# First stage of a fused attention and expert kernel: the slots a body later, the choice ahead of the shared product, the scatter calls regrouped behind the last root

## The chip, the cores and the metric

The kernel runs on one core of one Trainium2 chip. The metric is the device time of one execution in microseconds; lower is better. The core has five engines with a queue of instructions each: TensorE (PE in the profile; its weight loads are PEld), VectorE (DVE), ScalarE (ACT), GpSimd (POOL) and SyncE (SP, which here only issues DMA transfers). An engine works through its queue in order. It meets the others only at semaphores.

## The reference, cut to what matters

```python
x = x + xattn0(layernorm(x), ctx)      # softmax(q ctx^T) ctx, q = x W^T + b
x = x + ffn0(layernorm(x))             # shared expert + routed top-1 of 8 experts
x = x + xattn1(layernorm(x), ctx, ctx) # softmax attention with projected k, v
x = x + ffn1(layernorm(x))             # 8 binary trees of depth 7: silu(logits) on the taken path

# ffn0, x of (8192, 128):
logits = x @ gate_w                    # (8192, 8)
top_id, score = argmax(logits), sigmoid(max(logits))
routed = swiglu(x * score; expert top_id)
out = swiglu(x; shared) + routed
```

There are 64 batches of 128 rows of 128 numbers, all in fp32; the context has 120 keys for each batch.

## The kernel before, in words

The batches are worked in 16 groups of 4. The first stage (`phase_a`) does the first attention, the shared expert, the router's logits, and the projections that the third step needs. It is a software pipeline of 19 bodies, f = 0 to 18. Body f works for four groups at once: it starts group f (statistics, keys), does the attention of group g = f - 1, the shared expert's first product for group l = f - 2, and its second product for m = f - 3. Every engine has its own `a_body`, and the order of the calls in it is the order in that engine's queue. Nothing is reordered by a scheduler. `PS` is the PSUM memory, in 8 banks of 512.

The routed expert is done in two halves of 8 groups (32 tiles of 128 rows) each. For a half, these steps follow each other:

- `choose_tops` and `choose_experts` on DVE turn the logits into a one-hot of the chosen expert (`top`, `lead`, `best`, `onehot`).
- `a_count` on PE multiplies it with a triangle and with ones: how many rows stand ahead of a row, and in each tile.
- `a_first_slots` on DVE finds where each expert's rows begin, `a_slots` turns that into `POS`, the place of every row in a list sorted by expert, and signals `placed`.
- `score` on ACT takes the sigmoid of `top` and signals `scored`. `scale(k)` multiplies the rows of group k by it: for group 0 on POOL, for 1 to 7 on ACT (`SCALED_IN` says in which body), for 8 to 15 on ACT in `scale_late`. SP's `load_rows` brings those rows from DRAM into four buffers (`xsa`, `xsb`), used again and again, and into four late ones.
- `scatter` on POOL writes one tile of 128 rows to its places in `x_sorted` with an indirect DMA. There are 32 such calls for the first half in bodies 12 to 17, between the other work of POOL, and 32 for the second half behind `placed` 2.

POOL also takes the reciprocal root of the variances (`rstd`, the rows `ve` and `rs`), twice for each group; DVE's `normalise` waits for it. In body 16 there is no group f, and the only root is that of group 15's second norm.

The second stage runs the sorted rows, 20 units of 4 tiles, through the experts. SP loads unit r with `r_load` into `xs_in`; units 0 and 1 are loaded once every scatter of the first half has landed (`all_scattered(sp, HG)`). In body 18 PE turns unit 0 (`r_turn(0, 0)`) behind the last group's shared product (`s_down`) and ahead of `a_count(1)`, so the second half's counts, slots and scatters stand behind it too. The third stage does the second attention and the trees, in a loop over the 16 groups.

The table `ROUTES` names the router's step of a body: tops in body 7, experts in body 8 (`choose0`), both for the next quarter in body 10 (`choose1`), counts in body 11 (`count`). `CALLS` holds the numbers of the scatter calls. The first half of a body's calls stands between its two roots, the other half behind the second root. A buffer of rows is loaded again only when its four scatters have landed, and SP waits for that in its queue.

## Time and profile before

| What | Value |
|---|---|
| three runs, median (lowest to highest) | 837.2 us (835.5 to 839.71) |
| profiled execution | 840.62 us |
| its span | 837.4 us, 3.2 us less |
| PE busy | 785.9 us, 94% of the span |
| DVE, ACT, POOL busy | 650.4, 558.8, 251.1 us |
| first stage ends, first sorted unit turned on PE | 219.95 us after the span's start |

The profile is one execution. The chain of waits follows the work that ended last back to the start. The timeline lists the instructions of an engine with start and duration, where instructions of one kind are merged (x4), and in brackets how long the engine was idle before, and what released it. "issue" is a release that the profile can't name.

### The profile page before, as it was taken

The page shows a single profiled execution, that of the slowest core. Times are in us where ns is not written, and L with a number is a line of the kernel's source. Part 1 is how long each engine was busy: PE and PEld are TensorE (multiplying, and loading weights), DVE is VectorE, ACT ScalarE, POOL GpSimd, SP SyncE. Part 2 cuts the span into 40 slices and gives each one's busy share as a digit, 9 for nine tenths or more (in the row PEclk, how much of TensorE's full clock was granted, in tenths as well). Part 3 has the DMA queues.
Part 4 walks back from the last instruction along what each step waited for, and adds up shares of the span by engine and source line. Part 5 has one row for each costly group of instructions (what it writes and reads, how often), then busy time and mean ns, then how long its engine had stood idle before and what let it go on. Part 6 is the DMA issues. An engine that isn't in the chain of part 4 may idle for free.

```text
span 837.4 us, 15003 instructions
## 1 busy us (share of the span) xinstructions
PE 785.9 (94%) x4424; PEld 635.5 (76%) x4464; DVE 650.4 (78%) x1730; ACT 558.8 (67%) x1007; POOL 251.1 (30%) x293
## 2 busy tenths in 40 slices
PE   5899997897878899999999999999999999999997
PEld 4788776776768899967777777777777777777775
DVE  5888889887824467778888888888888888888774
ACT  3577667685524434467777778678777777877765
POOL 2332322666265225112321331242133133211000
PEclk9999999999879899999999999999999999999999
DMA  6337784562523334100000000000000000000000
GB/s 170 87 112 197 200 238 135 165 176 72 161 85 105 92 110 115 51 25 11 26 27 0 25 25 0 25 25 19 6 25 25 0 25 25 16 11 13 13 1 25
DMA packets 91175, 55.79 MB, mean 67 GB/s; under 512 B 13439, under 2 KB 87799, under 8 KB 90999
## 3 DMA queue, kind: packets, MB, share of 16 engines
q1 hardware_dynamic: 75440, 41.29, 17.6%
q0 software_dynamic: 4096, 8.40, 3.5%
q10 hardware_dynamic: 11591, 5.50, 2.4%
q8 instruction: 25, 0.41, 0.2%
q14 instruction: 23, 0.19, 0.1%
HBM read 32.23 MB, written 22.94 MB: 66 GB/s over the span
## 4 chain that ended last, share of the span: by engine, by line
PE 76%; DVE 10%; ACT 7%; issue 4%; another core or an unknown queue 2%; DMA 0%; DVEq 0%; ACTq 0%; SPq 0%
PE PS L870 7%; PE PS L1124 7%; PE PS L855 7%; PE PS L1146 7%; PE PS L1148 7%; PE PS L1147 6%; PE PS L1126 6%; PE PS L1125 6%; PE PS L1068 4%; PE PS L1135 4%; PE PS L878 3%; PE PS L1133 2%; PE PS L1051 2%; PE PS L1036 2%; DVE xn L1205 2%
## 5 line engine op out<-in xcount | busy, mean ns | idle before, releaser
L812 ACT ACTIVATE sil<-PS,b_in_c 128x512 f32<-128x512 f32 x256 | 162.2, 685 | 92.2 <-PE PS L1133 60.7
L1591 DVE TENSOR_TENSOR sil_l<-sil,sil_h 128x512 fp32r<-128x512 f32 x256 | 164.8, 686 | 48.5 <-ACT sil_h L820 48.5
L542 POOL TENSOR_TENSOR ve<-mv,eps 128x4 f32<-128x4 f32 x64 | 19.7, 309 | 444.1 <-DVE mv L1199 442.6
L820 ACT ACTIVATE sil_h<-sil 128x512 fp32r<-128x512 f32 x224 | 128.9, 631 | 0.0
L1146 PE MATMUL PS<-sil_h,wout_l 128*128 128x512 f32 x256 | 118.8, 464 | 1.7 <-DVE sil_l L1591 1.6
L1124 PE MATMUL PS<-x4T_h,win_l 128*128 128x512 f32 x256 | 102.4, 400 | 0.9 <-ACT sil L812 0.4
L1148 PE MATMUL PS<-sil_h,wout_h 128*128 128x512 f32 x256 | 100.6, 393 | 0.0
L1147 PE MATMUL PS<-sil_l,wout_h 128*128 128x512 f32 x256 | 100.2, 391 | 0.0
L1126 PE MATMUL PS<-x4T_h,win_h 128*128 128x512 f32 x256 | 100.0, 391 | 0.0
L1125 PE MATMUL PS<-x4T_l,win_h 128*128 128x512 f32 x256 | 99.9, 390 | 0.0
L1575 DVE TENSOR_SCALAR dec<-PS,b_in_c 128x512 bf16<-128x512 f32 x128 | 95.4, 745 | 3.9 <-PE PS L1126 2.1
L870 PE MATMUL PS<-xsT,w_now 128*128 128x128 f32 x624 | 80.2, 282 | 3.4 <-issue 1.9
L604 POOL DMA_INDIRECT ys<-y_sorted,idx x64 | 72.0, 1125 | 27.8 <-issue 15.1
L870 PEld LDWEIGHTS PS<-xsT,w_now 128*128 128x128 f32 x624 | 76.0, 198 | 5.3 <-issue 4.7
L544 POOL TENSOR_TENSOR rs<-ve,neg_half 128x4 f32<-128x4 f32 x64 | 70.7, 1105 | 5.0
L769 ACT ACTIVATE sg<-PS 128x512 f32<-128x512 f32 (+1 forms) x40 | 23.4, 586 | 63.3 <-PE PS L870 45.6
L1194 DVE BATCH_NORM_STATS2 st<-X 128x6 f32<-128x128 f32 (+1 forms) x256 | 55.6, 280 | 9.5 <-DMA X<-in_x 4.5
L1265 DVE COPY w_now<-WGU 128x512 f32 x78 | 30.8, 436 | 41.0 <-PE PS L870 23.5
L1146 PEld LDWEIGHTS PS<-sil_h,wout_l 128*128 128x128 f32 x256 | 48.3, 189 | 18.7 <-DVE sil_l L1591 4.1
L1124 PEld LDWEIGHTS PS<-x4T_h,win_l 128*128 128x128 f32 x256 | 48.0, 188 | 16.5 <-issue 3.9
L1148 PEld LDWEIGHTS PS<-sil_h,wout_h 128*128 128x128 f32 x256 | 48.0, 188 | 11.2
L1126 PEld LDWEIGHTS PS<-x4T_h,win_h 128*128 128x128 f32 x256 | 48.0, 188 | 10.5
(174 smaller groups left out, 1575.1 us busy)
## 6 DMA issues: line engine op xcount, KB each, us to landing
x_sorted<-zeros SPq DMA_DIRECT2D x4, 1280.0 KB, 6.8
xs_in<-x_sorted SPq DMA_DIRECT2D x20, 256.0 KB
y_sorted<-yo ACTq DMA_DIRECT2D x18, 256.0 KB
X<-in_x SPq DMA_DIRECT2D x16, 256.0 KB
rows<-xn SPq DMA_DIRECT2D x16, 256.0 KB
out<-res SPq DMA_DIRECT2D x16, 256.0 KB
ctxT<-in_ctx_t SPq DMA_DIRECT2D x16, 240.0 KB
ctx_rows<-in_ctx_kv SPq DMA_DIRECT2D x16, 240.0 KB
```

The lines of the kernel that those rows point to most:

```text
L604: pool.indirect_dma_start(tile(ys[u], j), None, y_sorted[half], bass.IndirectOffsetOnAxis(ap=idx[:, u, j:j + 1], axis=0)).then_inc(y_in[u] ...
L812: act.activation(tile(sil[p % 2], c, W), bank(2 * (p % 2) + c), ACT.Silu, bias=b_in_c[:, 2 * p + c:2 * p + c + 1]).then_inc(t_silu, 1)
L820: act.activation(tile(sil_h[p % 2], c, W), tile(sil[p % 2], c, W), ACT.Copy).then_inc(t_hi, 1)
L870: i = pe.matmul(tile(bank(1 + 2 * v + t), n), tile(w_now[v], 2 * FC * t + n), tile(xsT[u], 2 * v + t), start=True, stop=True)
L1124: pe.matmul(dst, lo, x4T_h, start=True, stop=False, skip_group_check=True)
L1125: pe.matmul(dst, hi, x4T_l, start=False, stop=False, skip_group_check=True)
L1126: i = pe.matmul(dst, hi, x4T_h, start=False, stop=True, skip_group_check=True)
L1146: pe.matmul(bank(4), lo, act_h, start=(p == 0 and c == 0), stop=False)
L1147: pe.matmul(bank(4), hi, act_l, start=False, stop=False)
L1148: pe.matmul(bank(4), hi, act_h, start=False, stop=(p == TREES - 1 and c == 1)).then_inc(t_out, 1)
L1575: dve.tensor_scalar(dec[p % 2], bank(2 * (p % 2)), b_in_c[:, 2 * p:2 * p + 1], 0.0, ALU.add, ALU.is_gt).then_inc(t_dec, 1)
L1591: dve.tensor_tensor(tile(sil_l[p % 2], c, W), tile(sil[p % 2], c, W), tile(sil_h[p % 2], c, W).bitcast(F32), ALU.subtract).then_inc(t_lo, 1)
```

## The change

- `a_slots(0)` leaves the end of body 11 (route `count`) and stands in body 12 (new route `slots`), behind DVE's first `normalise` and ahead of the attended rows (`X<-PS,srec,X`).
- `score(0)` on ACT and the scaling of group 0 on POOL move from body 11 to body 12. `scale` on ACT waits for `scored` as well.
- In bodies 7, 8 and 10 DVE chooses ahead of the shared expert's product (`s_act<-s_act,PS`), not behind it; in body 10 the tops stand ahead of it and the experts behind.
- `CALLS` is now a table of three numbers for a body: the calls from the first to the second stand between the roots, those up to the third behind the second root. The calls of bodies 12 to 17 are 3, 6, 6, 6, 6, 5 (before 6, 6, 6, 6, 6, 2).
- In body 16 all six calls stand behind the root.
- POOL's wait for `zeroed` and `placed` stands behind the scaling of group 0. ACT scales group 2 in body 13 (before 12) and group 5 in body 15 (before 14).

```diff
-        ROUTES = {HG - 1: "choose0", HG: "choose0", HG + 2: "choose1", HG + 3: "count", NG + 1: "pack", NG + 2: "all"}
+        ROUTES = {HG - 1: "choose0", HG: "choose0", HG + 2: "choose1", HG + 3: "count", HG + 4: "slots",
+                  NG + 1: "pack", NG + 2: "all"}
-        CALLS = [0, 6, 12, 18, 24, 30, 32]
-        SCALED_IN = {HG + 4: (1, 2), HG + 5: (3,), HG + 6: (4, 5), HG + 7: (6,), HG + 8: (7,)}
+        CALLS = [(0, 0, 3), (3, 6, 9), (9, 12, 15), (15, 18, 21), (21, 21, 27), (27, 32, 32)]
+        SCALED_IN = {HG + 4: (1,), HG + 5: (2, 3), HG + 6: (4,), HG + 7: (5, 6), HG + 8: (7,)}
@@ POOL, a_body
-                if calls and calls[0] == 0:
-                    pool.wait_ge(zeroed, 16 * 4)
-                    pool.wait_ge(placed, 1)
-                half = (len(calls) + 1) // 2
-                for t in calls[:half]:
+                for t in range(calls[0], calls[1]):
                     scatter(t, 0, HG)
...
-                for t in calls[half:]:
-                    scatter(t, 0, HG)
-                if route == "count":
+                if route == "slots":
                     pool.wait_ge(scored, 1)
                     scale(0)
+                    pool.wait_ge(zeroed, 16 * 4)
+                    pool.wait_ge(placed, 1)
+                for t in range(calls[1], calls[2]):
+                    scatter(t, 0, HG)
@@ ACT, scale and a_body
+                act.wait_ge(scored, 1)
...
+                    if route == "slots":
                         score(0)
@@ DVE, a_body
+                if route == "slots":
+                    a_slots(0)
                 if g is not None:
                     dve.wait_ge(a_rec, g + 1)
...
+                if route == "choose0":
+                    choose_tops(0) if f == HG - 1 else choose_experts(0)
+                if route == "choose1":
+                    choose_tops(1)
                 if l is not None:
                     dve.wait_ge(s_sil, l + 1)
                     dve.tensor_tensor(s_act, s_act, PS[:, 6 * 512:8 * 512], ALU.mult).then_inc(s_act_d, 1)
-                if route == "choose0":
-                    choose_tops(0) if f == HG - 1 else choose_experts(0)
                 if route == "choose1":
-                    a_choose(1)
-                if route == "count":
-                    a_slots(0)
+                    choose_experts(1)
```

DVE's queue from the end of body 11 into body 12, before (`first_slot` ends `a_first_slots`; `slot` to `POS` is `a_slots`; `nmax` opens body 12; the last row is the attended rows):

```order
L1428 TENSOR_SCALAR first_slot<-first_slot 128x8 [waits route_step]
L1349 TENSOR_TENSOR s_act<-s_act,PS 128x1024 [waits s_sil,route_step]
L1435 TENSOR_TENSOR slot<-upto,first_slot 128x256
L1436 TENSOR_TENSOR lead<-ahead,slot 128x256 [waits route_step]
L1439 CAST POS<-posf 128x32 [waits route_step]
L1283 TENSOR_REDUCE nmax<-PS 128x4 [waits a_s_ps]
L1205 TENSOR_SCALAR xn_79<-X,mv,rs 128x128 [waits a_rs2,a_rows,a_x2T_ps]
L1205 TENSOR_SCALAR xn<-X,mv,rs 128x128 [waits a_rs1,a_xnT_ps]
L1330 SCALAR_TENSOR_TENSOR X<-PS,srec,X 128x128 [waits a_pv_ps,a_rec]
```

The same place in the changed kernel:

```order
L1431 TENSOR_SCALAR first_slot<-first_slot 128x8 [waits route_step]
L1356 TENSOR_TENSOR s_act<-s_act,PS 128x1024 [waits s_sil,route_step]
L1284 TENSOR_REDUCE nmax<-PS 128x4 [waits a_s_ps]
L1206 TENSOR_SCALAR xn_79<-X,mv,rs 128x128 [waits a_rs2,a_rows,a_x2T_ps]
L1206 TENSOR_SCALAR xn<-X,mv,rs 128x128 [waits a_rs1,a_xnT_ps]
L1438 TENSOR_TENSOR slot<-upto,first_slot 128x256
L1439 TENSOR_TENSOR lead<-ahead,slot 128x256 [waits route_step]
L1442 CAST POS<-posf 128x32 [waits route_step]
L1333 SCALAR_TENSOR_TENSOR X<-PS,srec,X 128x128 [waits a_pv_ps,a_rec]
```

The slots have moved from in front of `nmax` to a place behind the body's second `normalise`. The line numbers of the changed kernel are a few higher or lower.

POOL's queue from the second root of body 15 to the second half's first call, before (`xsa` and `xsb` are the row buffers; with their own numbers):

```order
L542 TENSOR_TENSOR ve<-mv,eps 128x4 [waits a_mv2]
L566 DMA x_sorted0<-xsa1_61,POS 5120x128 [waits k_act] x3
L566 DMA x_sorted0<-xsb0_68,POS 5120x128 [waits k_act] x3
L542 TENSOR_TENSOR ve<-mv,eps 128x4 [waits a_mv2]
L544 TENSOR_TENSOR rs<-ve,neg_half 128x4 [waits a_ve2]
L566 DMA x_sorted0<-xsb0_68,POS 5120x128 [waits k_act]
L566 DMA x_sorted0<-xsb1_69,POS 5120x128 [waits k_act] x4
L566 DMA x_sorted1<-xsa0_60,POS 5120x128 [waits placed,k_late]
```

The same place in the changed kernel:

```order
L543 TENSOR_TENSOR ve<-mv,eps 128x4 [waits a_mv2]
L567 DMA x_sorted0<-xsa0_60,POS 5120x128 [waits k_act] x2
L567 DMA x_sorted0<-xsa1_61,POS 5120x128 [waits k_act]
L543 TENSOR_TENSOR ve<-mv,eps 128x4 [waits a_mv2]
L545 TENSOR_TENSOR rs<-ve,neg_half 128x4 [waits a_ve2]
L567 DMA x_sorted0<-xsa1_61,POS 5120x128 [waits k_act] x3
L567 DMA x_sorted0<-xsb0_68,POS 5120x128 [waits k_act] x4
L567 DMA x_sorted0<-xsb1_69,POS 5120x128 [waits k_act] x4
L567 DMA x_sorted1<-xsa0_60,POS 5120x128 [waits placed,k_late]
```

The last root (the later row `ve<-mv,eps` with a_mv2) had 1 + 4 calls of the first half behind it, and three calls in front of it in its own body. Now it has 3 + 4 + 4 calls behind it and none in front in its body.

## Rows read from the trace of the kernel before

**Rows 1.** Page, chain that ended last: share of the span by engine
```profile
PE 76%; DVE 10%; ACT 7%; issue 4%; another core or an unknown queue 2%; DMA 0%; DVEq 0%; ACTq 0%; SPq 0%
```

**Rows 2.** Timeline, DVE, bodies 8, 11, 12: start, duration (us), line, operation, [idle before]
```profile
91.72 1.22 DVE L1349 TENSOR_TENSOR s_act<-s_act,PS 128x1024 f32<-128x1024 f32 x1 [0.94 <-ACT s_act L730]
...
93.93 0.66 DVE L1283 TENSOR_REDUCE nmax<-PS 128x4 f32<-128x480 f32 x1
...
141.74 0.17 DVE L1427 TENSOR_TENSOR first_slot<-tile_end,tiles_f 128x8 f32<-128x8 f32 x1
141.94 1.07 DVE L1428 TENSOR_SCALAR first_slot<-first_slot 128x8 f32<-128x8 f32 x1
...
144.18 0.42 DVE L1435 TENSOR_TENSOR slot<-upto,first_slot 128x256 f32<-128x256 f32 x1
...
146.28 0.65 DVE L1283 TENSOR_REDUCE nmax<-PS 128x4 f32<-128x480 f32 x1
...
149.76 0.69 DVE L1278 TENSOR_TENSOR X<-X,PS 128x512 f32<-128x512 f32 x1 [0.50 <-PE PS L878]
...
154.44 1.13 DVE L1330 SCALAR_TENSOR_TENSOR X<-PS,srec,X 128x128 f32<-128x128 f32 x4 [1.46 <-PE PS L977]
```

**Rows 3.** The same, PE, at the start of bodies 8, 9, 12
```profile
95.67 0.66 PE L855 MATMUL PS<-WA,xn 128*128 128x128 f32 x4 [0.87 <-DVE xn L1205]
...
107.77 0.66 PE L855 MATMUL PS<-WA,xn 128*128 128x128 f32 x4 [0.56 <-DVE xn L1205]
...
143.98 1.04 PE L916 MATMUL PS<-ctxT,W0C 128*128 128x480 f32 x2 [1.80 <-ACT KT L679]
...
148.01 0.66 PE L855 MATMUL PS<-WA,xn 128*128 128x128 f32 x4 [2.10 <-DVE xn L1205]
```

**Rows 4.** The same, ACT: body 11, body 14, routed stage
```profile
138.45 1.28 ACT L653 ACT_TABLE_LOAD   x1
...
139.88 0.58 ACT L723 ACTIVATE xnT<-PS 128x512 f32<-128x512 f32 x1
...
176.38 1.28 ACT L659 ACTIVATE xsa<-xsa,SCORE 128x128 f32<-128x128 f32 x4 [0.46 <-DMA xsa<-rows]
...
241.01 0.60 ACT L769 ACTIVATE sg<-PS 128x512 f32<-128x512 f32 x1 [6.58 <-remote]
...
272.59 0.60 ACT L769 ACTIVATE sg<-PS 128x512 f32<-128x512 f32 x1 [7.18 <-remote]
```

**Rows 5.** The same, POOL: score scaling, last root, scatter calls
```profile
141.94 1.04 POOL L551 TENSOR_TENSOR xsa<-xsa,SCORE 128x512 f32<-128x512 f32 x1
...
205.93 0.20 POOL L542 TENSOR_TENSOR ve<-mv,eps 128x4 f32<-128x4 f32 x1 [4.18 <-DVE mv L1199]
...
207.45 1.03 POOL L566 DMA_INDIRECT x_sorted<-xsb,POS  x1 [0.20 <-issue]
...
212.58 0.96 POOL L566 DMA_INDIRECT x_sorted<-xsb,POS  x1 [0.30 <-issue]
```

**Rows 6.** The same, SP's queue: a row load, first sorted loads
```profile
173.19 0.45 SPq L466 DMA_DIRECT2D xsa<-rows  x1
...
214.99 0.91 SPq L501 DMA_DIRECT2D xs_in<-x_sorted  x2
```

**Rows 7.** Tile late_rows, loads issued behind these: time to landing
```profile
DMA to landing us min/median/max: 5.3/5.5/5.8
```

**Rows 8.** Timeline, PE, end of first stage, start of the second
```profile
216.91 3.25 PE L878 MATMUL PS<-SD,s_act 128*128 128x128 f32 x16 [2.06 <-DVE s_act L1349]
219.95 1.06 PE L855 MATMUL PS<-WA,xs_in 128*128 128x128 f32 x4
...
221.75 2.02 PE L870 MATMUL PS<-xsT,w_now 128*128 128x128 f32 x16
...
246.98 3.75 PE L870 MATMUL PS<-xsT,w_now 128*128 128x128 f32 x16 [1.14 <-DVE ract L1514]
```

**Rows 9.** Windows: length, busy PE, PEld, DVE, ACT, POOL, granted clock, DMA share, GB/s
```profile
216.00:226.00 10.00, 8.94 (x59) 8.17 (x59) 7.76 (x23) 6.48 (x14) 0.00 (x0) 0.83 0.91 249
```

More of the change, by code:

```diff
@@ L359, in phase_a @@
                 body(stage(f), stage(f - 1), stage(f - 2), stage(f - 3), f % 2,
-                     range(CALLS[k], CALLS[k + 1]) if 0 <= k < len(CALLS) - 1 else (), ROUTES.get(f),
+                     CALLS[k] if 0 <= k < len(CALLS) else (0, 0, 0), ROUTES.get(f),
                      SCALED_IN.get(f, ()))
@@ L567, in scatter, with a_body @@
                                         tile(rows_of(k), t % G), None).then_inc(scattered[v], 16)
-            def a_body(f, g, l, m, u, calls=(), route=None, rows=()):
+            def a_body(f, g, l, m, u, calls=(0, 0, 0), route=None, rows=()):
                 if f is not None:
                     rstd(0, f, a_mv1, a_ve1, a_rs1)
-                if calls and calls[0] == 0:
-                    pool.wait_ge(zeroed, 16 * 4)
-                    pool.wait_ge(placed, 1)
-                half = (len(calls) + 1) // 2
-                for t in calls[:half]:
+                for t in range(calls[0], calls[1]):
                     scatter(t, 0, HG)
@@ L687, in take_gates, with a_body @@
                 act.activation(LGT[at:at + 32, :], bank(2, W, 32), ACT.Copy).then_inc(a_gT, 1)
-            def a_body(f, g, l, m, u, calls=(), route=None, rows=()):
+            def a_body(f, g, l, m, u, calls=(0, 0, 0), route=None, rows=()):
                 if m is not None and route != "all":
@@ L916, in project_keys, with a_body @@
                 pe.matmul(bank(0, KW), W0C[:, :], ctxT[u], start=True, stop=True).then_inc(a_k0_ps, 1)
-            def a_body(f, g, l, m, u, calls=(), route=None, rows=()):
+            def a_body(f, g, l, m, u, calls=(0, 0, 0), route=None, rows=()):
                 if g is not None:
@@ L1278, in add_shared, with a_body @@
                     dve.tensor_tensor(row, row, bank(3), ALU.add).then_inc(s_add, 1)
-            def a_body(f, g, l, m, u, calls=(), route=None, rows=()):
+            def a_body(f, g, l, m, u, calls=(0, 0, 0), route=None, rows=()):
                 if g is not None:
```

## The prediction

> **What bounds the kernel now.** I read the chain of waits first: PE holds 76% of it, DVE 10% and ACT 7% [rows 1]. So time is won or lost where PE stands idle, and I looked for that with the timelines of the engines, around the two places the change touches: bodies 7 to 13, and the seam to the second stage. In the first place the reader is to see that PE waits for DVE: at the start of bodies 8, 9 and 12 it idles 0.87, 0.56 and 2.10 us until DVE has normalised the next group, and 1.80 us in body 12 until ACT has taken the keys out [rows 3]. In the second place the reader is to see a chain that PE doesn't wait for yet, but nearly: last root on POOL at 205.93, five scatter calls from 207.45, the last ending at 212.58 + 0.96 = 213.54, SP's load of the first sorted unit at 214.99 [rows 5, 6], and PE turning that unit at 219.95 without an idle bracket, right behind the last shared product [rows 8].
>
> All times below are set against the profiled execution (840.62 us, 3.2 us over its span). It lies 3.4 us above the median of 837.2, so I carry the difference over to the median.
>
> **Part 1: the choice ahead of the shared product.** In body 7 DVE idles 0.94 us until ACT's silu is there, then multiplies from 91.72, ends at 92.94, and only after the tops comes to `nmax` at 93.93 [rows 2]. The tops take 0.99 us and fit the idle 0.94 nearly exactly. PE, which idled 0.87 us for this [rows 3], gets it: -0.87. Body 8's experts do the same, and PE idled 0.56 in front of body 9, so -0.56 (no more, since then ACT's keys hold PE). In body 10 DVE comes to the product with no such idle, and the swap moves one second of DVE work in front of another; PE's product starts later, inside its own idle before body 11. I take 0 (bounds 0 and +0.5). Sum -1.4.
>
> **Part 2: slots, score and scaling leave body 11.** Three things shift there. The five slot instructions, from 144.18 to 146.28, are 2.10 us in front of `nmax` [rows 2]. POOL's scaling of group 0 runs from 141.94 for 1.04 us, and beside it DVE's `first_slot`, 8 numbers for each partition, takes 1.07 us [rows 5, 2]; the row of the same size in front of it takes 0.17 [rows 2], so I count 0.9 us. ACT's table load for the sigmoid and the sigmoid itself fill 138.45 to 139.88, in front of `xnT` [rows 4]; without them silu and the keys come 1.4 us earlier, so that the product need not wait for silu (it starts when `first_slot` ends, 0.9 us earlier) and PE's 1.80 us wait for the keys shrinks. Together `nmax` of body 12 comes 2.1 + 0.9 = 3.0 us earlier.
>
> The slots are not gone. They now stand in front of the attended rows at 154.44, where DVE idled 1.46 us for PE [rows 2]. PE comes 3 us earlier too, since it waited for DVE's `normalise`, so these waits of DVE (1.46, and 0.50 ahead of the shared add at 149.76) go, and the slots fill them: 3.0 - 2.1 + 1.46 + 0.50 = 2.9 us earlier for the attended rows. POOL's addition to V now falls beside DVE's `normalise` there, for which I take 0.1 off. So part 2 gives -2.8 us, with bounds -1.4 (only ACT's and POOL's share) and -3.2.
>
> The Trainium skill, in "SBUF — State Buffer", section "SBUF: two separate sides", says that DVE in its fast modes and GpSimd take a shared port pair as an exclusive lock, and the other fully blocks. The 1.07 us beside 1.04 us agrees. The same section has a trap that speaks against the change: scatter calls issued from GpSimd can't write their descriptors while DVE copies from SBUF to SBUF. The calls from 207.45 to 212.58 keep one pace beside DVE's work, so the sum doesn't hold it; by that rule the last calls, which now meet DVE's copies of expert weights, would take some 2.5 us more each (its own example is 620 ns alone and 3100 ns beside a copy), and with one such call the estimate would be +5.8 us instead of +3.3.
>
> **Part 3: the calls.** Before, five calls stood behind the last root, now eleven. From 207.45 to 212.58 there are four steps [rows 5], 1.28 us each, so six more calls take +7.7 us. POOL idled 4.18 us ahead of the root at 205.93 for DVE's statistics [rows 5], so having the root ahead of the calls brings nothing: it waited for DVE, not for the calls. That idle only grows, by the three calls taken out in front of it. What is queued behind: SP waits in its queue for all 32 scatters and then issues the load of units 0 and 1, six loads of rows, and unit 2; PE's turn of unit 0 has `a_count(1)`, the second half's slots and all its 32 calls behind it.
>
> So the load of unit 0 comes at 214.99 + 7.7 - 4.2 (parts 1 and 2) = 218.5. Its landing is not in the trace. The lower bound is a load of the same 256 KB on a quieter queue, issued at 173.19 and releasing ACT at 176.38 [rows 6, 4]: 3.2 us. The upper bound is 5.8 us, for late rows issued behind it in the busiest stretch, 249 GB/s [rows 7, 9]. It is the first issued of eight, so I take 3.5 us, near the lower one. PE turns unit 0 at 222.0, not at 219.95: +2.0 us (+1.7 to +4.3). Of the 7.7 us, 219.95 - 214.99 - 3.5 = 1.5 fall on slack, 4.2 eat the gain whole, and 2.0 are left.
>
> **Part 4: PE's clock.** PE finishes the last shared product 4.2 us earlier, near 216, and idles some 6 us. After idle of 2.06 us and more its matmuls ran at the lower level: 16 of `s_down` took 3.25 us, and 16 of the expert product took 3.75 us at 246.98 against 2.02 us at 221.75 [rows 8]; the granted clock of 216 to 226 was 0.83 [rows 9], the mean of a stretch at 1.2 GHz and one at 2.4. In the old run the turn itself was still in the slow stretch. In the new one turn, counts and the first expert product are behind a fresh idle, so the product costs up to 3.75 - 2.02 = 1.7 us more. ACT and DVE wait for PE there. I take +1.3 (0 to +2.3, if the slow stretch lasts into the next unit).
>
> **Part 5: the regrouped loads and scalings.** Call 3 stands half a body later, so the reload of buffer 0 in SP's queue, the context load behind it and the others come some 4 us later; each is read about a body after (12.1 us, from 95.67 to 107.77 [rows 3]). ACT scales group 5 a body later, as the second of two scalings in the wait for its next evacuation. Both hidden, 0; if one cover is gone, +1 us. The load for group 9 now waits for calls 21 to 23, behind the last root, but is read behind unit 0's turn: 0.
>
> **Sum.** -1.4 - 2.8 + 7.7 - 1.5 + 1.3 = +3.3 us. Profiled execution 843.9, median 840.5 us.
>
> **Rivals.**
> - *The gate costs more.* The landing is nearer 5.8 us (+2.3), or part 2 gives only 1.4 us (+1.4), or the clock takes 2.3 (+1.0): +5 to +8, median 843.5. For it: eight loads in flight and 0.91 of the DMA engines' time [rows 9]. Against: this load is the first of the eight issued.
> - *The gate is loose.* It would be if unit 0's load landed before PE ends the last product, 14.3 us behind the root (201.7 to 216). But 1.5 + 11 calls (10 x 1.28 + 0.96) + 1.4 to SP's load + 3.2 of landing are 19.9 us. What can happen is the good end of every bound: part 2 at 3.2, landing 3.2, no clock lost, +1.2, median 838.4.
> - *Slack given back later* (the other sign). ACT waits 6.58 and 7.18 us ahead of 241.01 and 272.59 for PE [rows 4], and no row names what PE waits for; it looks like its supply of instructions. If the 6 us that PE now idles at the seam let that supply run ahead, the first stall goes: +3.3 - 6.6, median 833.9; with both gone, 826.7. It decides from the point where the supply gained at the seam is over the 4.2 + 3.3 us needed to get below 833. Against: both stalls lie among the second half's scatters, which shift together with PE, and the second is 50 us behind the seam. The Trainium skill's "Runtime: NRT & Kernel Launch", section "Instruction fetch mechanics", says that an engine's sequencer fetches its next page of instructions on its own DMA queue while it works on the present one, mostly hidden; no row here shows the fetch. By the same mechanism a stall can grow, to 847.
> - *The change doesn't do what it says:* having the root ahead of the calls doesn't make it earlier. That is in the sum.
>
> **How the numbers follow.** What this kernel's runs can tell from no change is about 0.5%, 4.2 us: 833.0 to 841.4. My forecast (+1 to +6, its own range 838 to 843.5) has 0.58, of which 0.36 lies within the bound and 0.22 above it. The costlier gate has 0.13, all slower. The good end of all bounds has 0.05, within. Slack given back has 0.17: 0.12 faster, 0.05 within. A grown stall has 0.05, slower, and 0.02 is left for no effect. That is 0.12 faster, 0.48 the same, 0.40 slower. The range 833.5 to 846.5 leaves out the faster part and the tail of the costlier gate.
>
> **What would show it.** Step 1: PE's idle ahead of bodies 8 and 9 gone. Step 2: `first_slot` at 0.2 us, `nmax` of body 12 at 141.9, PE's 2.10 us wait gone, the last root near 201.7. Step 3: eleven calls in a row, the last ending near 217, SP's load near 218.5, and PE with an idle bracket of 5 to 6 us ahead of unit 0's turn, near 222.0. Step 4: a granted clock near 0.5 behind it. If the turn stands before 219.95, the prediction fails at part 3; if the last root is not 4 us earlier, at parts 1 and 2.

## The result, and the profile after

| | changed kernel | kernel before |
|---|---|---|
| four runs each, same chip: median (lowest to highest) | 845.78 us (844.83 to 846.65) | 838.37 us (835.5 to 839.71) |
| profiled execution, its span | 844.83, 841.8 us | 840.62, 837.4 us |

The ratio is 1.0102, with a 95% interval of 1.0074 to 1.013: slower by 7.4 us. I had forecast 840.5 us, +3.3. The sign of the sum was right and its size was less than half; the direction had a chance of 0.40 only.

Later runs fell on five other chips. They gave two kinds of times, and the reading of every trace below depends on it. On three chips (called free here) the kernel before takes 816 us, on the first and two others (called starving) 838 to 843. Each chip was seen in one session only, so whether this belongs to the chip or to the moment isn't shown. The difference lies almost wholly in stalls, mostly in the routed stage: from the turn of unit 0 to that of the last unit PE takes 126.5 us in the trace of before on the first chip and 107.3 on a free one, and behind it the two are within 0.4 us of each other.

The timeline of the changed kernel on the first chip, DVE in bodies 11 to 13, against [rows 2]:

```profile
139.91 0.17 DVE L1431 TENSOR_SCALAR first_slot<-first_slot 128x8 f32<-128x8 f32 x1
...
141.26 0.65 DVE L1284 TENSOR_REDUCE nmax<-PS 128x4 f32<-128x480 f32 x1
...
144.58 0.69 DVE L1279 TENSOR_TENSOR X<-X,PS 128x512 f32<-128x512 f32 x1 [0.34 <-PE PS L879]
...
154.04 0.65 DVE L1284 TENSOR_REDUCE nmax<-PS 128x4 f32<-128x480 f32 x1
...
161.02 1.15 DVE L1206 TENSOR_SCALAR xn<-X,mv,rs 128x128 f32<-128x128 f32 x4 [1.72 <-POOL rs L545]
```

`first_slot` takes 0.17 us, not 1.07; `nmax` of body 12 starts at 141.26, not 146.28, and PE's wait for it in body 12 is 0.44 us, not 2.10. Body 13's `nmax` begins at 154.04. Then something new: DVE waits 1.72 us for POOL's root in body 13. POOL's own queue shows why, and then the end of its first-half work, against [rows 5]:

```profile
153.77 1.04 POOL L552 TENSOR_TENSOR xsa<-xsa,SCORE 128x512 f32<-128x512 f32 x1
155.82 1.19 POOL L567 DMA_INDIRECT x_sorted<-xsa,POS  x1 [1.01 <-POOL xsa L552]
157.32 0.97 POOL L567 DMA_INDIRECT x_sorted<-xsa,POS  x1 [0.30 <-issue]
158.59 0.96 POOL L567 DMA_INDIRECT x_sorted<-xsa,POS  x1 [0.30 <-issue]
159.57 0.22 POOL L543 TENSOR_TENSOR ve<-mv,eps 128x4 f32<-128x4 f32 x1
159.87 1.04 POOL L545 TENSOR_TENSOR rs<-ve,neg_half 128x4 f32<-128x4 f32 x1
...
200.43 0.20 POOL L543 TENSOR_TENSOR ve<-mv,eps 128x4 f32<-128x4 f32 x1 [6.47 <-DVE mv L1200]
...
201.94 1.03 POOL L567 DMA_INDIRECT x_sorted<-xsa,POS  x1 [0.20 <-issue]
...
214.81 0.96 POOL L567 DMA_INDIRECT x_sorted<-xsb,POS  x1 [0.30 <-issue]
```

The scaling of group 0 now stands in this queue ahead of the three calls, and `ve` at 159.57 comes behind the third call. Behind the last root eleven calls start between 201.94 and 214.81, one each 1.29 us in the mean. SP's queue and PE at the seam, against [rows 6, 8], then ACT in the routed stage, against [rows 4]:

```profile
217.20 0.91 SPq L502 DMA_DIRECT2D xs_in<-x_sorted  x2
```
```profile
213.63 3.68 PE L879 MATMUL PS<-SD,s_act 128*128 128x128 f32 x16 [3.42 <-DVE s_act L1356]
220.13 0.76 PE L856 MATMUL PS<-WA,xs_in 128*128 128x128 f32 x4 [2.83 <-DMA xs_in<-x_sorted]
...
221.62 3.11 PE L871 MATMUL PS<-xsT,w_now 128*128 128x128 f32 x16
```
```profile
246.31 0.60 ACT L770 ACTIVATE sg<-PS 128x512 f32<-128x512 f32 x1 [9.30 <-remote]
...
257.84 0.60 ACT L770 ACTIVATE sg<-PS 128x512 f32<-128x512 f32 x1 [4.01 <-PE PS L871]
...
284.43 0.60 ACT L770 ACTIVATE sg<-PS 128x512 f32<-128x512 f32 x1 [7.56 <-remote]
```

The load is issued at 217.20, unit 0 is turned at 220.13 behind 2.83 us of idle (landing 220.13 - 217.20 = 2.9 us), and its first expert product takes 3.11 us, not the 2.02 of [rows 8]. But 220.13 is only 0.2 us behind the 219.95 of before. The other 4.2 us between the two spans (841.8 - 837.4 = 4.4) come later: ACT waits for more than 4 us three times (9.30, 4.01 and 7.56) where it did so twice (6.58 and 7.18), and the last unit is turned at 351.00, where it was at 346.47. Windows of the changed kernel, with the columns of [rows 9]:

```profile
216.00:226.00 10.00, 7.08 (x42) 6.19 (x42) 4.78 (x15) 3.11 (x5) 0.00 (x0) 0.78 0.84 224
236.00:246.00 10.00, 6.33 (x26) 5.32 (x27) 0.69 (x1) 0.60 (x1) 6.49 (x7) 0.75 0.26 79
```

In 236 to 246 PE is busy 6.33 us of ten at a clock of 0.75, with DMA at 0.26: nothing is saturated, DVE and ACT stand still with it (0.69 and 0.60 us busy), and POOL issues the second half's calls (6.49).

### The profile page after: what moved, and what is told of

It is laid out like the page before. It is cut to its first block, busy times and chain, and to the rows that moved or that the text cites. A ratio compares the mean times of both kernels' runs of the same rounds, so it can differ in the third digit from the quotient of the medians.

```text
span 841.8 us, 15051 instructions
## 1 busy us (share of the span) xinstructions
PE 790.2 (94%) x4464; PEld 637.0 (76%) x4464; DVE 648.3 (77%) x1730; ACT 558.6 (66%) x1007; POOL 250.6 (30%) x293
## 4 chain that ended last, share of the span: by engine, by line
PE 73%; DVE 8%; issue 7%; ACT 7%; another core or an unknown queue 3%; DMA 1%; POOL 1%; SPq 0%; DVEq 0%; ACTq 0%; POOLq 0%
PE PS L871 7%; PE PS L1125 7%; PE PS L1147 7%; PE PS L1127 7%; PE PS L1126 7%; PE PS L1149 7%; PE PS L1148 7%; PE PS L856 6%; PE PS L1069 4%; PE PS L1134 3%; PE PS L1136 3%; PE PS L1052 2%; PE PS L1037 2%; DVE xn L1206 2%
## 5 line engine op out<-in xcount | busy, mean ns | idle before, releaser
L871 PE MATMUL PS<-xsT,w_now 128*128 128x128 f32 x624 | 82.6, 287 | 3.3 <-issue 2.7
L871 PEld LDWEIGHTS PS<-xsT,w_now 128*128 128x128 f32 x624 | 78.4, 203 | 4.1 <-issue 3.5
L603 POOL DMA_INDIRECT ys<-y_sorted,idx x64 | 72.6, 1134 | 27.9 <-issue 15.1
```

The costliest lines, as they stand in the source:

```text
L603: pool.indirect_dma_start(tile(ys[u], j), None, y_sorted[half], bass.IndirectOffsetOnAxis(ap=idx[:, u, j:j + 1], axis=0)).then_inc(y_in[u] ...
L871: i = pe.matmul(tile(bank(1 + 2 * v + t), n), tile(w_now[v], 2 * FC * t + n), tile(xsT[u], 2 * v + t), start=True, stop=True)
```

## The experiments

CALLS is the table of scatter calls. Theory A: the eleven calls behind the last root delay unit 0's load (the gate), and PE runs slowly behind the idle. Rival R: the loss is a third stall in the routed stage. Theory S, on the stalls: the second half's scatters cause them. Times in two traces can be set against each other in two ways, from the start of the span or from body 7's `nmax`, which is the last common point ahead of the change. Executions of one kernel begin body 7 up to 1.9 us apart, so both are given where they differ.

### One part at a time, on a free chip

**Gate alone** (before, with calls grouped so that eleven stand behind the last root, and the loops that read the table; slots, score and choice as before):

```diff
-        CALLS = [0, 6, 12, 18, 24, 30, 32]
+        CALLS = [(0, 3, 6), (6, 9, 12), (12, 15, 18), (18, 21, 21), (21, 21, 27), (27, 32, 32)]
```

> The kernel before with nothing changed but the groups of the scatter calls: eleven instead of five stand behind the last root (body 15 has three fewer, body 16 has all six behind its root). The front stays as before, so the last root stays near 205.9. Theory A (a gate at the seam): the last call ends 6 x 1.28 = 7.7 us later, near 221.2, SP's load near 222.7, landing 2.9 us later as in the changed kernel, so PE turns unit 0 near 225.6 instead of 219.95: +5.7 us at the seam, and about that or a few us more in the time (843 to 848). Theory B (the seam doesn't matter, the loss comes from PE's stalls in the routed stage): the time moves by the number and length of those stalls and not with the seam; under it this kernel could stay at the time of before. Theory C (the regrouped calls disturb something in bodies 12 to 16): bodies 13 to 16 would get longer in this kernel.

822.95 us against 815.72, ratio 1.010 (1.008 to 1.012): +7.2. PE at the seam:

```profile
212.55 3.47 PE L877 MATMUL PS<-SD,s_act 128*128 128x128 f32 x16 [1.93 <-DVE s_act L1348]
221.59 1.09 PE L854 MATMUL PS<-WA,xs_in 128*128 128x128 f32 x4 [5.57 <-DMA xs_in<-x_sorted]
```

PE waits 5.57 us for the load. Counted from body 7's `nmax`, the load is issued 7.8 us later than in the trace of before on another free chip (137.9 against 130.2): this is the 7.7 us of part 3. The front was to stay, and did: the last root comes 121.3 us behind body 7's `nmax`, against 121.2.

**Choice alone** (before, with the choice ahead of the shared product in bodies 7, 8, 10):

```diff
+                if route == "choose0":
+                    choose_tops(0) if f == HG - 1 else choose_experts(0)
+                if route == "choose1":
+                    choose_tops(1)
                 if l is not None:
                     dve.wait_ge(s_sil, l + 1)
...
-                if route == "choose1":
-                    a_choose(1)
+                if route == "choose1":
+                    choose_experts(1)
```

> The kernel before with only the choice moved ahead of the shared product in bodies 7, 8 and 10. Part 1 of the prediction said -1.4 us for the front; the changed kernel shows nmax of body 8 at 92.62 instead of 93.93 and of body 9 at 103.94 instead of 106.04, so -2.1. I expect the last root near 203.8, PE's turn of unit 0 two us earlier (near 217.9, the calls behind the root move with it), and the whole 1 to 3 us faster, unless PE's stalls in the routed stage move.

814.91 us, ratio 0.9993 (0.998 to 1.0006): no measurable change. But the last root comes 118.0 us behind body 7's `nmax` (198.89 - 80.86), where the kernel before takes 121.2 (200.99 - 79.84, its trace on another free chip). So the choice moves the front by 3.1 us. How much of that reaches the end isn't settled: the last unit is turned at 320.01 against 321.30 in that trace of before, which is 1.3 us earlier, or 2.3 counted from body 7, and the medians differ by 0.8, which is within the interval. Where the 3.1 us come from is told apart below.

**Gate opened** (the changed kernel with seven calls behind the last root):

```diff
-        CALLS = [..., (21, 21, 27), (27, 32, 32)]
+        CALLS = [..., (21, 25, 25), (25, 32, 32)]
```

> The changed kernel with one edit: four calls of body 16 stand ahead of the last root, seven behind it instead of eleven. The last root stays near 200.4 (POOL idles 6.5 us ahead of it). Theory A: the last call ends near 210.7, the load of unit 0 is issued near 212.1 and lands near 215, before PE ends the last shared product near 217.3, so PE turns unit 0 without a wait: the turn near 217.3 or below against 220.1, 3 us or more earlier than the changed kernel and 2.6 earlier than before, and no slow clock behind a new idle (1 us more). If nothing else happens: faster than before by 2.5 to 6 us. Theory B (stalls of PE in the routed stage are what made the changed kernel slower): the seam gains its 3 us, and the time lies still near or above the kernel before, since the stalls stay at 10 to 16 us in sum.

814.46 us, ratio 0.9988 (0.9979 to 0.9997). Unit 0 is turned at 213.82 with 0.64 us of idle. Four calls stand ahead of the last root again, and POOL still idles 1.03 us in front of that root, so they cost it nothing; the whole loss is back. It was run on three more chips, below.

**Gate closed, second half's scatters left out** (the changed kernel without the second half's 32 calls, and with the waits that counted them cut to the first half; the rows of groups 8 to 15 are left out of the routed result):

```diff
-            for t in range(B0[1], B):
-                scatter(t, 1, NG)
```

> The changed kernel without the 32 scatter calls of the second half (its rows in DRAM stay zero, and nothing waits for them). The question is what makes PE issue matmuls one by one for 4 to 9 us, two or three times between 230 and 286. Theory S (the indirect scatters, on their queue or in their descriptors, starve PE's supply of instructions): without them there is no such stall, the routed stage is 12 to 16 us shorter, about 830 to 833 us. Theory P (the stalls belong to places in PE's instruction stream or to the loads and stores of SP and ACT): they stay, at about 237, 257 and 280, and the time stays near 845.

821.56 us, ratio 1.0068 (1.0049 to 1.0086), unit 0 turned at 219.62 behind 5.50 us of idle. But no kernel on that chip had a stall, so it told nothing on theory S. Beside the changed kernel's 820.68 and 821.37 us on two other free chips it says that there the second half's calls cost next to nothing.

### The two kernels side by side on a free chip

> The kernel before as it is, for its trace. Theory A expects, where PE isn't starved, the last root near 202 (a gate with five calls behind it), unit 0's turn at 214 to 217 behind the last shared product with 0 to 1 us of idle, so 3 to 6 us ahead of the changed kernel's 219.66, and a time of 815 to 817. Where PE is starved, two or three stalls and a turn near 219 to 220, since the front is late as well.

> The changed kernel as it is. Where PE isn't starved: ratio 1.006 to 1.008 as before (821 to 822 us). Where it is: if the change itself adds a stall, three stalls and a ratio near 1.010 as on the first chip; if the number of stalls is chance, a ratio of 1.000 to 1.005 and runs that scatter over 5 us, as in the second pair.

815.94 us (ratio to the shared runs of before 1.0003, 0.9991 to 1.0016) against 820.68 (1.0062, 1.0042 to 1.0082). The changed kernel on another free chip gave 821.37 us, ratio 1.007 (1.0057 to 1.0083). PE of the kernel before at the seam, then of the changed kernel, same chip:

```profile
210.93 3.33 PE L878 MATMUL PS<-SD,s_act 128*128 128x128 f32 x16 [1.93 <-DVE s_act L1349]
214.05 1.01 PE L855 MATMUL PS<-WA,xs_in 128*128 128x128 f32 x4
...
215.79 2.02 PE L870 MATMUL PS<-xsT,w_now 128*128 128x128 f32 x16 [0.18 <-issue]
217.65 0.60 PE L855 MATMUL PS<-WA,xs_in 128*128 128x128 f32 x4
```
```profile
212.30 2.05 PE L879 MATMUL PS<-SD,s_act 128*128 128x128 f32 x16 [1.93 <-DVE s_act L1356]
219.74 1.09 PE L856 MATMUL PS<-WA,xs_in 128*128 128x128 f32 x4 [5.38 <-DMA xs_in<-x_sorted]
...
221.56 3.43 PE L871 MATMUL PS<-xsT,w_now 128*128 128x128 f32 x16
224.82 0.60 PE L856 MATMUL PS<-WA,xs_in 128*128 128x128 f32 x4
```

With theory A's expectations in hand, the whole sum can be read, with the queues of SP and POOL: the last root moves from 200.99 to 200.13, the load from 210.01 to 216.94, the turn from 214.05 to 219.74 (+5.7), unit 1's turn from 217.65 to 224.82 (+7.2; the first product takes 3.43 us against 2.02), and the last unit's turn from 321.30 to 327.93 (+6.6). The spans differ by 818.3 - 811.9 = 6.4, the medians by 4.7. The pair of traces overstates the loss: the one of before is the fastest of its kernel's nine runs (814.91), and it begins body 7 at 79.84, where the other begins it at 81.61. Counted from there the turn of unit 0 comes 3.9 us later, unit 1's 5.4, the last unit's 4.9, and the end 4.6, like the medians. The trace of the changed kernel on the other free chip began body 7 at 79.75, took 13.87 us for body 11 (12.21 here) and turned unit 0 at 219.66, which is +5.6 or +5.7. The seam costs 3.9 to 5.7 us, by the execution. My expectation for the root of before (near 202) was 1 us too late.

### The two kernels on a second starving chip

> The changed kernel, unchanged. Theory A (the gate at the seam and the slow clock behind it): last root near 200, PE's idle ahead of unit 0 near 5.5 us, the turn 3.5 to 4 us later than in the kernel before of this call, the first expert product at half clock for 1.5 to 2 us more, and the time 5 to 6.5 us over the kernel before. Theory B (the loss is in further stalls of the routed stage): from unit 1 to unit 19 this kernel takes several us longer than the kernel before.

845.74 us, ratio 1.0037 (0.9991 to 1.0082): inconclusive. The kernel before ran beside it as a kernel of its own for its trace (840.98 in two runs, ratio 0.9988, 0.9925 to 1.0052). Its ACT timeline of the routed stage:

```profile
244.56 0.60 ACT L769 ACTIVATE sg<-PS 128x512 f32<-128x512 f32 x1 [9.39 <-remote]
...
257.69 0.60 ACT L769 ACTIVATE sg<-PS 128x512 f32<-128x512 f32 x1 [5.46 <-remote]
...
280.73 0.60 ACT L769 ACTIVATE sg<-PS 128x512 f32<-128x512 f32 x1 [5.46 <-remote]
```

The kernel before has three stalls here, where it had two on the first chip; its seven runs beside it lie between 837.55 and 844.94. So a third stall needs no change, and rival R isn't shown. It isn't ruled out as an effect on how often one comes: of the seven starving traces that have the second half's calls, the three with eleven calls behind the last root take 130.9 to 132.9 us from unit 0's turn to the last unit's, the four others 126.0, 126.5, 127.7 and, in this one, 130.6. On a free chip the changed kernel takes 108.2 there and the one before 107.3. Unit 0 is turned at 219.07 here and at 219.98 in the changed kernel: at the seam this pair loses 0.9 us, or 0.2 counted from body 7, and not the 3.5 to 4 that I expected.

### What makes the stalls, and the opened gate, on a third starving chip

> The changed kernel with seven calls behind the last root. Where PE isn't starved: ratio 0.998 to 1.000, as three times before. Where it is (kernel before at 837 to 845 us): theory A expects a ratio of 0.993 to 1.001, under the changed kernel's 1.004 to 1.010; if the loss there came from the stalls alone, 1.003 to 1.010.

> The changed kernel without the second half's 32 scatter calls (those rows are left out of the output). Where PE is starved, theory S (their traffic starves it) expects no stall between 230 and 290 us and 822 to 830 us; its rival the same two or three stalls and 838 to 846 us. Where no kernel has stalls it tells nothing, ratio 1.006 to 1.007 as before.

Gate open: 839.0 us against 838.86, ratio 1.0013 (0.9995 to 1.0031), between what I expected by theory A (up to 1.001) and by its rival (from 1.003). The changed kernel itself did not run on this chip. Without the second half's calls: 822.1, ratio 0.9803 (0.9777 to 0.9829). PE in the first, where the clearest stall begins, then windows of both:

```profile
239.64 0.27 PE L1069 MATMUL PS<-WD,ract 128*128 x1 [1.03 <-issue]
241.05 0.37 PE L1069 MATMUL PS<-WD,ract 128*128 x1 [1.14 <-issue]
242.44 0.60 PE L1069 MATMUL PS<-WD,ract 128*128 x2 [1.02 <-issue]
```
```profile
236.00:246.00 10.00, 4.10 (x17) 3.31 (x17) 2.72 (x6) 3.32 (x8) 5.76 (x6) 0.74 0.22 67
246.00:290.00 44.00, 39.27 (x303) 38.66 (x302) 17.49 (x39) 17.01 (x38) 19.13 (x20) 0.87 0.35 103
```
```profile
236.00:246.00 10.00, 10.00 (x93) 10.00 (x92) 5.01 (x10) 5.80 (x15) 0.00 (x0) 1.00 0.27 80
246.00:290.00 44.00, 44.00 (x397) 44.00 (x396) 23.43 (x53) 20.91 (x44) 2.13 (x3) 1.00 0.34 97
```

With the gate open PE issues matmuls singly or in pairs, with about 1 us between them that nothing in the trace explains ("issue"), and is busy 4.10 of 10 us with the DMA engines at 0.22. Without those calls PE is busy 10.00 of 10 and 44.00 of 44, and the time is that of the same kernel on the free chips (821.56, 820.9 and 820.95 in three studies). So theory S holds for the stalls of the routed stage, on the one starving chip where it was tried: they need these calls, and a chip of this kind. The gate-open kernel shows what they cost: 839.0 us here, 814.2 to 814.7 on the free chips, 24 to 25 us. Not all of it is in the routed stage: its unit 0 is turned at 217.43, where a free chip has 213.2 to 213.8, after one wait of PE of 5.38 us ahead of a shared product at 204.13, where all free chips have 2.55. The second half's calls begin only at 226.74, so they don't cause that one. What the traces of the starving chips have in common is the first half's calls of body 16:

| kernel, its starving chip | calls in body 16 ahead of the last root | PE's wait there | body 16's `nmax` to the last root |
|---|---|---|---|
| before, first | 3 | 3.50 us | 10.9 us |
| before, second | 3 | 4.42 | 11.2 |
| one call ahead of body 13's root, second (below) | 5 | 3.53 | 12.6 |
| gate open, third | 4 | 5.38 | 12.2 |
| changed, first | 0 | 2.55 | 9.4 |
| changed, second | 0 | 2.56 | 9.4 |
| PE kept busy, second (below) | 0 | 2.55 | 9.4 |
| no second half's calls, third | 0 | 2.56 | 9.4 |

With calls ahead of that root DVE and ACT stand idle and go on within 0.02 us of each other (in the opened gate at 200.30 and 200.29, after 4.13 and 3.74 us). Without them, and on every free chip with or without them, PE waits 2.55 us. In eight traces the split is clean, yet no run varied it alone on one chip. By it the regrouping brings the last root 1.5 to 3.2 us forward on a starving chip, and nothing on a free one, where up to four calls ahead of it leave the 9.3 us as they are. What isn't shown is the path: the calls' descriptors, their writes, or POOL's part in it, and why three of six chips don't show it. The Trainium skill's "Runtime: NRT & Kernel Launch", section "Instruction fetch mechanics", has the fetch of the next page of instructions on a DMA queue of its own; that it is held up by the scatters would fit, and no row here shows such a fetch waiting.

The opened gate on its four chips, and the changed kernel as it is (where a kernel was repeated on a free chip, I expected what its first run there gave):

| kernel, free or starving | ratio to before (95%) | us |
|---|---|---|
| gate open, free | 0.9988 (0.9979 to 0.9997) | 814.46 |
| gate open, free | 0.9989 (0.9979 to 0.9998) | 814.72 |
| gate open, free | 0.9985 (0.9976 to 0.9995) | 814.21 |
| gate open, starving | 1.0013 (0.9995 to 1.0031) | 839.0 |
| changed, free | 1.007 (1.0057 to 1.0083) | 821.37 |
| changed, free | 1.0062 (1.0042 to 1.0082) | 820.68 |
| changed, starving (first chip) | 1.0102 (1.0074 to 1.013) | 845.78 |
| changed, starving | 1.0037 (0.9991 to 1.0082) | 845.74 |

### Two attempts on what the opened gate leaves

**One call ahead of body 13's root**, with eight behind the last root:

```diff
-        CALLS = [(0, 0, 3), (3, 6, 9), (9, 12, 15), (15, 18, 21), (21, 21, 27), (27, 32, 32)]
+        CALLS = [(0, 0, 1), (1, 4, 7), (7, 10, 13), (13, 16, 19), (19, 24, 24), (24, 32, 32)]
```

> The changed kernel with other groups of calls: one call instead of three in body 12, three between any two roots in bodies 13 to 15, five ahead of the last root, eight behind it. In the changed kernel DVE waits 1.72 us for the root of body 13, which stands on POOL behind the scaling of group 0 and three calls. If that is the cause, the wait goes, nmax of body 14 comes 1.7 us earlier than in the changed kernel, and the last root too, near 198. The last call then ends near 209.5, unit 0 lands near 214, little after PE's last shared product, so the turn is near 214 and the time 5 to 7 us below the changed kernel and about 1 to 2 below before. If DVE alone bounds body 13, the wait stays in another form and nothing is gained there.

842.19 us, ratio 1.000 (0.9945 to 1.0055), on the second starving chip. DVE's wait for POOL's root in body 13 is gone and `nmax` of body 14 comes at 164.82, 1.8 us before the 166.64 of the changed kernel beside it; by body 16 it is 190.50 against 190.81. The last root, expected near 198, comes at 203.13, 3.0 us later than the changed kernel's (the wait of the table above). The load still comes 0.8 us earlier, at 216.12, and unit 0 is turned without a wait at 219.93, against 219.98: what the gate gave back, the front had lost. The time settles nothing, within an interval of 1.1%.

**The same with six behind the last root** (calls 1, 6, 7, 7, 5, 6), on a free chip:

> The changed kernel with calls of 1, 6, 7, 7, 5, 6: one call ahead of body 13's root, six behind the last root. It joins what two earlier runs showed apart: the wait for POOL's root in body 13 goes (1.7 us) and the gate is open. Theory A expects 0 to 2 us under the one with seven behind the last root, 813 to 814 where PE isn't starved. If DVE makes up the 1.7 us in bodies 15 and 16 anyway, the two are equal.

815.03 us, ratio 0.9989 (0.998 to 0.9998), equal to the one with seven on the same chip (814.72). Its last root is at 198.61, its load at 209.08, 1.4 us ahead of the other's 210.52, and unit 0 is turned without a wait, right behind the last product: the gate is no longer last there, so an earlier load brings nothing. With five calls ahead of it the root itself is held up here: POOL has no idle in front of it, and it comes 10.2 us behind body 16's `nmax`, where the other free traces have 9.3.

**PE kept busy at the seam**: six matmuls ahead of unit 0's turn whose result is never read.

```diff
                     pe.wait_ge(a_k1, NG)
+                    for _ in range(6):
+                        pe.matmul(bank(5, KW), WM[:, :], cols(KT, 0, KW), start=True, stop=True)
                     r_turn(0, 0)
```

> The changed kernel with six matmuls more (merged weights times the first group's keys, into a bank that nothing reads), ahead of unit 0's turn, where PE idles 3 to 5.5 us for the load. They change no result. If the slow clock behind the idle costs 1.5 to 2 us, the first expert product (16 matmuls) takes near 2.0 us instead of 3.1 to 3.75, and the time is 1.5 to 2 us below the changed kernel. If ACT and DVE bound the first units, the matmuls are faster and the time stays.

842.17 us, ratio 1.001 (0.9965 to 1.0054). PE turns unit 0 at 221.61, 1.6 us later than the changed kernel beside it (219.98), and unit 1 at 224.81 against 224.42: 3.2 us for the unit and not 4.4. The first expert product takes 2.02 us against 2.86, and the granted clock of 216 to 226 is 0.97 against 0.80. So the clock at the seam is worth 1.2 us, and this way of keeping it costs 1.6 us at the turn. The medians (842.17 against the changed kernel's 845.74) lie within the scatter of this chip and don't decide which is more.

## Why the prediction was wrong, step by step

Two terms failed, one on each kind of chip. On the first chip, where the forecast was made, it was the term that isn't written down: that everything behind the seam shifts as a whole. The turn moved by +0.2 us where I had +2.0, and 4.2 us more came behind it where I had 1.3: 0.8 of them stand at unit 1's turn, as the slow clock, and the other 3.4 are in the stalls of the routed stage. On the free chips, where no stall hides the seam, it was the gain in front of the gate: 4.2 us forecast, 2.6 measured behind body 7. The mechanism of the seam was right. That the sum had the right sign on the first chip is mostly luck: 3.4 of the 4.4 us between its two spans come from stalls that the sum held constant.

- **Part 1, the choice, -1.4.** Too small. Bodies 7 to 9 gave what I read: 12.39 and 12.10 us before became 11.39 and 11.31 between `nmax` starts with the choice alone, both on free chips, -1.8. But body 12 went from 12.67 us (12.65 in the gate-alone kernel on the choice-alone's own chip) to 11.18, another -1.5, with a higher granted clock of PE. Windows of the kernel before on a free chip, then of choice alone:

```profile
144.00:152.00 8.00, 6.04 (x31) 5.43 (x31) 6.29 (x23) 4.89 (x19) 3.63 (x5) 0.79 0.55 172
```
```profile
144.00:152.00 8.00, 6.53 (x45) 5.89 (x46) 7.13 (x28) 6.04 (x20) 4.32 (x5) 1.00 0.58 182
```

  The clock is at the higher level throughout (1.00) where it was a mean of both (0.79). What differs ahead of it is the swap in body 10, which I priced at zero: PE's idle before body 11, 2.06 us in one piece before, is 0.59 and 1.22 us. The idles of body 12 are the same (1.79 and 1.96 in both). That the one explains the other is argued, since no run varied this idle alone.
- **Part 2, the slots, -2.8.** It was right at body 12 and wrong at the last root. On the free chip `nmax` of body 12 comes 64.6 us behind that of body 7 before (144.42 - 79.84) and 60.0 after (141.62 - 81.61), 4.6 earlier, where I had 1.4 + 3.0. The last root comes 118.5 us behind body 7's `nmax`, 2.6 earlier and not 4.2 (118.5 in three gate-open traces too): less than the choice alone gives. Body 12 itself, with the slots in it, now takes 12.8 us (154.41 - 141.62) where choice alone has 11.2, and body 13, which waits for POOL, 13.0 where it has 11.15. So what the slots save in body 11 (12.2 us against 15.1) is paid back by 3.4 us in the two bodies behind it: beside the choice, part 2 gave nothing.
- **Part 5, hidden, 0.** This failed in body 13: the scaling of group 0 and three calls stand ahead of a root that DVE waits 1.7 us for. I followed the queues of SP and ACT there and not POOL's own root.
- **Part 3, the seam, +2.0.** The six calls cost 7.7 us as read. The terms were: load 218.5 (measured 217.20), landing 3.5 (2.9), slack 1.5. The turn came at 220.13, +0.2 and not +2.0, because the root came 5.5 us earlier in this pair (205.93 to 200.43, 5.2 counted from body 7) and the landing was short; PE's idle was 2.83 us, not 5 to 6. The root passed my sign of being right (4 us earlier), but in part for a reason that I hadn't read: the kernel before lost 1.5 us in body 16 on this chip and not on a free one (10.9 us from `nmax` to root against 9.3), and another 1.0 in body 13 (12.1 against 11.1). The first loss is absent from every starving trace without calls ahead of that root. I had written that the root ahead of the calls brings nothing. PE, kernel before, the last wait but one ahead of the seam, first chip and then a free one:

```profile
207.01 1.85 PE L878 MATMUL PS<-SD,s_act 128*128 128x128 f32 x8 [3.50 <-DVE s_act L1349]
```
```profile
202.06 1.16 PE L878 MATMUL PS<-SD,s_act 128*128 128x128 f32 x8 [2.55 <-DVE s_act L1349]
```

  On a free chip the same step is +5.7: there the load comes 6.9 us later (7.7 less the 0.9 by which the last root is earlier in absolute time, the changed execution having begun body 7 1.8 us later), and the slack is 214.05 - 210.01 - 2.8 = 1.2. Counted from body 7 it is 7.7 - 2.6 - 1.2 = +3.9. Here the forecast broke on the free chips: +2.0 rests on 4.2 us of gain in front, and only 2.6 were there, with 1.2 of slack for 1.5. The six calls, the root and the landing are each read in the traces, and opening the gate gives the loss back, on three free chips.
- **Part 4, the clock, +1.3.** Right in kind and size: +1.5 between units 0 and 1 on the free chip, 0.9 left at the last unit's turn, and 1.2 by the kept-busy kernel. On the first chip the granted clock of 216 to 226 was 0.78 against 0.83 [rows 9].
- **The rest of the stage shifts as a whole.** That was assumed in the sum, and on the first chip it was wrong by 3.4 us (4.2 less the 0.8 of the clock). The trace before had two stalls, and I took them for a part of the kernel. They are not: an execution of it on the second starving chip has three, and no trace of a free chip has any. Whether the change makes a third one likelier is open. My rival "a stall can grow, to 847" had the place and nearly the time, and a chance of 0.05.
- **Rivals.** The good end of all bounds adds up to +1.3 and not +1.2. "The gate costs more" (+5 to +8) is what happens on the free chips (+4.7 to +5.1 in the medians, +7.2 alone), with a chance of 0.13. "Slack given back" fell: both traces of the changed kernel on starving chips have three stalls behind an idle of 2.83 and 2.94 us. Idle of 6 us never came there.

What stays open: how the 7.4 us of the first chip divide. The seam and its slow clock give 4.7 to 5.1 where nothing disturbs, but in the first chip's own pair of traces only 0.2 of the loss stands at the turn, 0.8 in the clock and 3.4 in the stalls, which differ between executions. One pair of traces can't tell a third stall that the change brings from one that was due anyway, and how the calls hold up the other engines on a starving chip isn't known.

## What to carry to other kernels

Count the instructions behind the last thing a gate waits for, on the queue that feeds it, and price them against the slack of the engine that waits at the gate; a front that comes earlier pays only what is left of that. Before a stall in the trace is used in a sum, see whether it is there in a second execution or on a second chip. See too what runs beside a queue that you thin out: on the starving chips every trace with calls in POOL's idle ahead of the last root had that root 1.5 to 3.2 us later. And when work moves into a body, follow the queue of each engine to the next result that another engine waits for, not only the one that was named.

## What the runs showed of the hardware that I had not expected

- The same program takes 816 us on three chips and 838 to 843 on three others (one session on each), with PE issuing matmuls one at a time while the DMA engines stand at 0.2 to 0.3. Without 32 indirect calls of POOL the starving chip gives 822.1 us, as the free ones do.
- The runs of the kernel before spread over 3.6 to 4.6 us on a free chip (some 20 runs each) and over 5.9 and 7.4 us on two starving ones (17 and 7 runs).
- A scatter call keeps its pace beside DVE: the eleven behind the last root take 0.95 to 1.12 us each in steps of 1.26 to 1.42, on either kind of chip. The trap that I weighed in part 2, from the Trainium skill's "SBUF — State Buffer", section "SBUF: two separate sides", didn't show: on the free chip the last of the eleven, at 214.50, ran into DVE's copy of expert weights from 214.96 and took 1.00 us, and of the second half's 32 calls there, the 16 that overlap such a copy took 0.95 to 1.08 us. This is the time on POOL's queue, not that of the transfer. The lock of the shared port did show again, by its absence: `first_slot` takes 0.17 us without POOL's scaling beside it, and took 1.07 with it.
